# Image line sums on TensorE, low row halves on Pool, token reloads issued at once, in a two-layer MetaFormer kernel

## The chip, the cores and the metric

The kernel runs on one core of a Trainium2 chip. The metric is the time of one execution on the device in microseconds (us), the median of several runs. The engines of the core are TensorE (PE, matmuls; its weight loads are shown as PEld), VectorE (DVE), ScalarE (ACT), GpSimd (POOL, here also called Pool) and SyncE (SP, which here issues most DMAs). They run their own instruction streams and meet only through semaphores.

## The reference

The input x is 16 images of 256 channels and 16 x 16 pixels. Two layers follow each other, each a convolution part and a mixture of experts on the 4096 pixels as tokens:

```
x = x + conv0(ln_c(x))              # ln_c: normed over the channels of a pixel
t = tokens(x)
t = t + ffn0(ln_t(t))               # 8 experts, 2 per token, hidden 512
x = from_tokens(t)
x = x + (weight1 @ ln_c(x) + bias1)
t = t + ffn1(ln_t(t))               # 8 experts, 2 per token, hidden 1024
```

conv0 works on groups of 8 channels. For each group it needs the mean and the maximum of every image row and every image column (`g.mean(axis=3)`, `g.mean(axis=2)` and the same with max), puts them through an 8 x 8 matrix, a bias and a sigmoid, and multiplies the image by the gates of its row and its column, once with the gates from the means (branch r = 0) and once with those from the maxima (r = 1). Statistics of the gated images, a softmax over the group and a mix of both branches follow.

In the experts a token's value is split into two float16 numbers, a high half and a low half (the rest), so that matmuls in float16 keep the accuracy.

## The kernel before

All instructions are written out by hand, engine by engine, with semaphores; the order on an engine is the order of the code. SBUF is laid out by hand too: `tok` holds the 32 token tiles of 128 x 256, `region` and `wreg` are reused from stage to stage.

**First convolution.** PE turns the images to tokens (L674), DVE takes statistics and norms each token tile into one of two buffers `xn` (L1245), PE turns it back (L664), ACT copies it to `g` (L960), channels by pixels: two blocks k of 128 channels, 16 images, 256 pixels. DVE then makes the line sums and line maxima into `line[:, r, k]`, for r = 0 (sum) and r = 1 (max), k = 0 and 1: rows by one reduction (L1273), columns by another (L1275), for r = 0, k = 0 by four additions that fold the image (L1279, L1281). PE multiplies each `line` by the gate matrix (L702), ACT makes the sigmoid (L976) between its sums of squares of expert weights (L968, `squares`). Gating is done in a row part (L256) and a column part (L261), by Pool for (r, k) = (0, 0), (0, 1), (1, 1) and by DVE for (1, 0). Pool starts (0, 0) and (0, 1) with their sigmoids; (1, 1) waits for `signed`, which DVE gives after it has multiplied the maxima's row gates by a sign (L1306). DVE takes `channel_stats` (L1296) of a gated block when it is there, in the order (0, 0), signs, its own gating (1, 0), then (0, 1), (1, 0), maxima (L1299), (1, 1), maxima.

**Between the layers.** Experts add their results to DRAM rows `rows_y`. SP waits for the last of these, reloads `tok` in eight DMAs of 512 KB (L395), of which the fifth to eighth each wait for one of the first four, and then loads raw expert weights (L320, L323). DVE takes statistics of each loaded tile (L1391).

**Second convolution and routing.** PE turns `tok` and multiplies by the weights (L903, L912); Pool adds the bias (L640), DVE adds the result (`result`, L1402) and takes statistics (L1408) for eight groups i of four tiles. `deviations(3, ..)` (L1216 to L1231) makes mean and 1/deviation for one half of the tiles at a time. ACT norms the tiles into `xn1` (L1026) and writes the high halves, scaled by 1024, into `rows` (L1030); `result_lows(i)` on DVE writes the low halves, `xn1 * 1024 - high` (L1415), two instructions per i. DVE does i = 0 to 3 between its results, and i = 4 to 7 after the routing chain (L1469 to L1535) and ahead of the lists (L1545, L1546), which PE sums (L790). ACT makes its rows of i = 4 to 7 behind the exponents of the routing chain. SP stores each i's rows to DRAM when both halves are there. When lists and stores are done, Pool fetches rows for the second layer's experts (L530).

## Time and profile before

| | |
|---|---|
| median of 3 runs | 1151.49 us (1150.26 to 1151.76) |
| profiled execution | 1151.33 us |
| its span in the trace | 1149.6 us |
| PE busy | 878.1 us (76%) |
| DVE busy | 750.4 us (65%) |
| ACT busy | 575.9 us (50%) |
| POOL busy | 503.5 us (44%) |

Busy time is the sum of an engine's instructions; the span runs from the first to the last instruction. A share of the span is an average over stages with different limits, so the rows below are taken from the stages that the change touches: the first convolution (about 5 to 145 us), the reload of tokens (604 to 624 us) and the second convolution with its routing (610 to 723 us).

### The profile page before, as it was taken

Reading aid. Unit: us, or ns where it says so; the run is one execution under the profiler, and the core shown is the slowest. Engines: PE = TensorE matmul, PEld = TensorE weight load, DVE = VectorE, ACT = ScalarE, POOL = GpSimd, SP = SyncE. Lnnn points to the kernel's source line nnn. Section 1 sums busy time; section 2 is a strip of 40 time slices with the busy share of each in tenths; the row PEclk is TensorE's granted clock in tenths of the full one; section 3 lists DMA queues with packets and bytes.
Section 4 is the critical chain, followed back from the end, with each engine's and each line's share of the span. In section 5 each row is a group of like instructions: output and inputs, shape, how many; then the busy total and the mean of one; then the engine's idle time right before and its main releaser. Section 6 shows DMA issues by size and latency. Waiting matters only on the chain.

```text
span 1149.6 us, 25137 instructions
## 1 busy us (share of the span) xinstructions
PE 878.1 (76%) x7033; PEld 740.0 (64%) x7033; DVE 750.4 (65%) x1814; ACT 575.9 (50%) x1246; POOL 503.5 (44%) x412
## 2 busy tenths in 40 slices
PE   5321085874499999999964826599999999999975
PEld 4201064861288888888853712488888888888863
DVE  5899878999544444444446799466766767766540
ACT  4538266884245445444451466354564554655433
POOL 1198000000247667666661410354655655656640
PEclk8655599895599999999996965799999999999996
DMA  8248265784255565555659136656555464434438
GB/s 266 74 146 296 105 199 195 244 282 116 49 135 105 97 101 99 98 101 96 102 91 297 38 110 157 120 127 142 120 101 143 73 146 78 69 73 78 74 59 292
DMA packets 196629, 152.24 MB, mean 132 GB/s; under 512 B 97056, under 2 KB 181480, under 8 KB 196456
## 3 DMA queue, kind: packets, MB, share of 16 engines
q1 hardware_dynamic: 156536, 108.48, 33.1%
q0 software_dynamic: 27472, 38.97, 20.5%
q10 hardware_dynamic: 12576, 4.26, 1.4%
q8 instruction: 20, 0.33, 0.1%
q14 instruction: 25, 0.20, 0.1%
HBM read 92.35 MB, written 39.91 MB: 115 GB/s over the span
## 4 chain that ended last, share of the span: by engine, by line
PE 35%; DMA 25%; DVE 18%; issue 11%; SPq 4%; ACT 3%; DVEq 1%; POOL 1%; ACTq 1%; POOLq 0%
PE bank L857 14%; PE bank L830 12%; DMA columns<-region 8%; DMA region<-rows_x,region 8%; SPq L419 3%; DMA rows_y<-region 3%; PE bank L912 2%; DVE columns L1296 2%; DVE region L1275 2%; DMA tok<-rows_y 2%; DVE region L1273 2%; PE bank L734 2%; DMA wreg<-in_L_ffn_w_dram 1%; DVE wreg L261 1%; PE bank L812 1%
## 5 line engine op out<-in xcount | busy, mean ns | idle before, releaser
L830 PE MATMUL bank<-columns,wreg 128*128 x3360 | 382.8, 274 | 26.9 <-DMA columns<-region 26.8
L830 PEld LDWEIGHTS bank<-columns,wreg 128*128 128x128 f16 x3360 | 330.2, 98 | 68.9 <-issue 28.5
L583 POOL DMA_INDIRECT rows_y<-region x140 | 242.0, 1729 | 161.0 <-ACT region L1172 99.2
L530 POOL DMA_INDIRECT region<-rows_x,region x148 | 155.9, 1053 | 252.2 <-DVE region L1572 141.4
L857 PE MATMUL bank<-wreg,region 128*128 128x256 f16 x1680 | 189.2, 273 | 10.4 <-DVE region L1701 10.3
L857 PEld LDWEIGHTS bank<-wreg,region 128*128 128x128 f16 x1680 | 163.5, 98 | 32.1 <-DVE region L1701 13.4
L1157 ACT ACTIVATE region<-bank,b_t,wreg 128x256 f32<-128x256 f32 x280 | 137.3, 558 | 25.9 <-PE bank L830 25.5
L1706 DVE TENSOR_TENSOR region<-region 128x256 f16<-128x256 f32 x140 | 50.1, 420 | 107.2 <-ACT region L1164 107.2
L1172 ACT ACTIVATE region<-region 128x256 f32<-128x256 f32 x70 | 31.7, 500 | 163.4 <-DVE region L1713 163.4
L1701 DVE SCALAR_TENSOR_TENSOR region<-region,wreg 128x512 f16<-128x512 f32 x140 | 105.2, 751 | 5.0
L845 PE MATMUL bank<-wreg,region 128*128 (+1 forms) x864 | 100.2, 273 | 1.9 <-ACT region L1164 1.9
L1698 DVE TENSOR_SCALAR region<-region,wreg 128x512 f16<-128x512 f32 x140 | 70.5, 503 | 41.5 <-ACT region L1157 41.5
L1152 ACT ACTIVATE region<-bank,fac 128x256 f32<-128x256 f32 x140 | 62.7, 473 | 62.6 <-PE bank L830 61.8
L845 PEld LDWEIGHTS bank<-wreg,region 128*128 128x128 f16 x864 | 84.4, 98 | 12.0 <-ACT region L1164 2.2
L1134 ACT ACTIVATE region<-bank,region 128x256 f32 x72 | 30.2, 470 | 100.5 <-DMA rows_y<-region 83.8
L790 PE MATMUL bank<-columns 128*128 128x160 f16 x128 | 38.7, 313 | 32.6 <-DVE columns L1546 28.2
L1695 DVE SCALAR_TENSOR_TENSOR region<-bank,fac,region 128x256 f32<-128x256 f32 x140 | 58.9, 477 | 7.0 <-ACT region L1152 7.0
L1713 DVE SCALAR_TENSOR_TENSOR region<-bank,wreg,region 128x512 f32<-128x512 f32 x35 | 26.3, 751 | 55.9 <-PE bank L857 38.9
L578 POOL COPY region<-routed 128x4 uint32 x70 | 59.9, 855 | 4.8 <-DMA region<-rows_x,region 3.0
L968 ACT ACTIVATE wreg<-wreg 128x1024 f32<-128x1024 f32 x56 | 58.5, 1051 | 2.0 <-DMA wreg<-in_L_ffn_w_dram 1.6
L1594 DVE SCALAR_TENSOR_TENSOR wreg<-wreg (+1 forms) x68 | 47.7, 747 | 6.8 <-ACT wreg L1109 4.3
L790 PEld LDWEIGHTS bank<-columns 128*128 128x128 f16 x128 | 13.3, 104 | 58.5 <-DVE columns L1546 49.2
(285 smaller groups left out, 1156.0 us busy)
## 6 DMA issues: line engine op xcount, KB each, us to landing
wreg<-in_L_ffn_w_dram SPq DMA_DIRECT2D x112, 512.0 KB, 6.0
rows_x<-region SPq DMA_DIRECT2D x16, 512.0 KB, 6.5
rows_y<-tok SPq DMA_DIRECT2D x16, 512.0 KB, 6.8
tok<-rows_y SPq DMA_DIRECT2D x16, 512.0 KB, 6.8
wreg<-in_x_dram SPq DMA_DIRECT2D x4, 1024.0 KB, 9.4
out_dram<-columns ACTq DMA_DIRECT2D x16, 256.0 KB, 2.4
region<-rows_x,region POOLq DMA_INDIRECT x148, 2.9
columns<-region SPq DMA_TRANSPOSE x148
```

The source lines that it names most:

```text
L530: nc.gpsimd.indirect_dma_start(x_bits[:, b, r, 0:C + 2], None, rows_x[f], bass.IndirectOffsetOnAxis(ap=row_list, axis=0)).then_inc(xr_load ...
L578: nc.gpsimd.tensor_copy(now[:, b], moves[:, bass.ds(2 * t, 2), :]).then_inc(lists_copied[f], 1)
L583: nc.gpsimd.indirect_dma_start(rows_y[f], bass.IndirectOffsetOnAxis(ap=now[:, b, g_, 1:2], axis=0), (y_pair[:, b], y_rows)[f][:, g_, :], N ...
L830: last = pe.matmul(to, block, x_cols[:, bass.ds(b, 1), :, xs_, k, :].rearrange("p j r n -> p (j r) n"), start=(k == 0 and ws_ + xs_ == 0), ...
L845: last = pe.matmul(yb[:, r * C:(r + 1) * C], lhs[:, r * P:(r + 1) * P], w2_of(c, ws_), start=(c == 0 and r == 0 and hs + ws_ == 0), stop=( ...
L857: last = pe.matmul(yb[:, r * C:(r + 1) * C], lhs[:, c, r * P:(r + 1) * P], v_s[:, e % 2, c // 2, 1, ws_, (c % 2) * C:(c % 2 + 1) * C], sta ...
L968: act.activation(chunk_in[:, n % SLOTS], chunk_in[:, n % SLOTS], ACT.Square, accum_out=to).then_inc(summed, 1)
L1152: act.activation(gate_act[:, h, (c % 2) * TILE:(c % 2 + 1) * TILE], zb[c][:, 0:TILE], ACT.Silu, scale=fac[f][:, 0, e:e + 1]).then_inc(silu ...
L1157: last = act.activation(gate_act[:, h, c * TILE:(c + 1) * TILE], zb[h][:, c * TILE:(c + 1) * TILE], ACT.Silu, bias=b1_t[:, e, 2 * h + c:2 ...
L1695: dve.scalar_tensor_tensor(half(hid[:, h], c), zb[c][:, TILE:2 * TILE], fac[f][:, 1, e:e + 1], half(gate_act[:, h], c), ALU.mult, ALU.mult ...
L1698: dve.tensor_scalar(to_hi, gate_act[:, h], fac[f][:, 1, e:e + 1], None, ALU.mult).then_inc(hi_ready[f], 1)
L1701: dve.scalar_tensor_tensor(to_lo, gate_act[:, h], fac[f][:, 1, e:e + 1], to_hi, ALU.mult, ALU.subtract).then_inc(lo_ready[f], 1)
```

## The change

There are three parts.

1. Norming of the first convolution writes all 32 token tiles to one array, `norm_rows`, instead of two turning buffers. The sums of image lines are made by PE: for each block k, image u and half h a matmul with the normed tile as weights and a selector `line_of` of 32 columns (16 rows, 16 columns of the image) as moving data. ACT copies the sums to `line[:, 0, k]`. DVE makes the selector at the start of the program and keeps the maxima alone.
2. `result_lows` moves from DVE to Pool, behind Pool's bias additions, as a plain subtraction. For this ACT writes `xn1` already scaled by 1024, with a `scaled` factor that DVE makes in `deviations(3, ..)`.
3. SP issues all eight token reloads with no wait among them (two semaphores take the place of one, so each load still has its own count), and waits for the last put `y_put[0]` last instead of first.

```diff
+        norm_rows = x_in.rearrange("p b k n -> p (b k n)").rearrange("p (t c) -> p t c", c=C)
+        line_of = region[:, 6144:6208].rearrange("p (h l) -> p h l", h=UT)
...
+        def tokens_in(f, i):
+            return (tok_loaded[i % 4], 16 + 16 * f) if (i < 4) == (f == 0) else (x_loaded[i % 4], 32 + 16 * f)
...
                 for i in range(HB):
...
-                    if i >= 4:
-                        sp.wait_ge(tok_loaded[f][i % 4], 16 + 16 * f)
                     sp.dma_start(tok[:, 4 * i:4 * i + 4, :], rows_y[f][i * 4 * P:(i + 1) * 4 * P].rearrange("(t p) c -> p t c", p=P)
-                                 ).then_inc(tok_loaded[f][i % 4], 16)
+                                 ).then_inc(tokens_in(f, i)[0], 16)
...
-            for waited, each, more in ((y_put[0], 16, 48), (y_put[1], 16, 16), (xr_loaded[0][0], 16, 48), (xr_loaded[1][0], 16, 48)):
+            for waited, each, more in ((xr_loaded[0][0], 16, 48), (xr_loaded[1][0], 16, 48), (y_put[1], 16, 16), (y_put[0], 16, 48)):
...
+            def result_lows(i):
+
+                for j in range(2):
+                    pool.wait_ge(rows_hi[j], HB + i + 1)
+                    at = rows[:, 4 * i + 2 * j:4 * i + 2 * j + UT, :]
+                    nc.gpsimd.tensor_tensor(at[:, :, C:2 * C], xn1[:, i % 4, j], at[:, :, 0:C], ALU.subtract
+                                            ).then_inc(rows_ready[j], 1)
...
+                    for i in range(HB):
+                        result_lows(i)
...
-            pairs(pe, turn_normed)
-
+            for i in range(HB):
+                turn_normed(i)
+
+            pe.wait_ge(lines_known, 1)
+            for k in range(KC):
+                for u in range(NB):
+                    for h in range(UT):
+                        last = pe.matmul(zb[2 + k][:, u * 2 * HW:(u + 1) * 2 * HW], norm_rows[:, UT * u + h, k * P:(k + 1) * P],
+                                         line_of[:, h], start=(h == 0), stop=(h == UT - 1))
+                last.then_inc(lines_known, 1)
             pe.wait_ge(bd_ready, 1)
             for r in range(2):
                 for k in range(KC):
-                    pe.wait_ge(lines_ready, 2 * (r * KC + k) + 2)
+                    if r == 0:
+                        pe.wait_ge(small_ready, 2 + k)
+                    else:
+                        pe.wait_ge(lines_ready, 2 * k + 2)
...
             squares(0, 4)
+            for k in range(KC):
+                act.wait_ge(lines_known, 2 + k)
+                act.activation(line[:, 0, k].rearrange("p b l -> p (b l)"), zb[2 + k][:], ACT.Copy).then_inc(small_ready, 1)
...
                 if s == 3:
-                    dve.scalar_tensor_tensor(m, m, -1.0, r, ALU.mult, ALU.mult).then_inc(half_normed, 1)
+                    chain(dve.tensor_scalar(scaled[:, at], r, XSCALE, None, ALU.mult))
+                    dve.scalar_tensor_tensor(m, m, -1.0, scaled[:, at], ALU.mult, ALU.mult).then_inc(half_normed, 1)
...
+            for h in range(UT):
+                dve.tensor_reduce(line_of[:, h, 8 * h:8 * h + 8], by_row, AX.X, ALU.add)
+                last = dve.tensor_reduce(line_of[:, h, HW:2 * HW], by_column, AX.X, ALU.add)
+            last.then_inc(lines_known, 1)
...
-                for j in range(2):
-                    dve.wait_ge(rows_hi[j], HB + i + 1)
-                    at = rows[:, 4 * i + 2 * j:4 * i + 2 * j + UT, :]
-                    dve.scalar_tensor_tensor(at[:, :, C:2 * C], xn1[:, i % 4, j], XSCALE, at[:, :, 0:C], ALU.mult, ALU.subtract
-                                             ).then_inc(rows_ready[j], 1)
```

On DVE this is the stretch from the gate matrix to the first statistics of a gated block, before. `region` holds the lines, `wreg` the images `g`.

```order
L1265 TENSOR_TENSOR region<-region 128x128
L1273 TENSOR_REDUCE region<-wreg 128x16x16
L1279 TENSOR_TENSOR region<-wreg 128x2048
L1279 TENSOR_TENSOR region<-region 128x16x64
L1279 TENSOR_TENSOR region<-region 128x16x32
L1281 TENSOR_TENSOR region<-region 128x16x16
L1273 TENSOR_REDUCE region<-wreg 128x16x16
L1275 TENSOR_REDUCE region<-wreg 128x16x16
L1273 TENSOR_REDUCE region<-wreg 128x16x16
L1275 TENSOR_REDUCE region<-wreg 128x16x16
L1273 TENSOR_REDUCE region<-wreg 128x16x16
L1275 TENSOR_REDUCE region<-wreg 128x16x16
```

The same stretch on DVE in the changed kernel, to its own gating.

```order
L1307 TENSOR_TENSOR region<-region 128x128
L1314 TENSOR_REDUCE region<-wreg 128x16x16
L1315 TENSOR_REDUCE region<-wreg 128x16x16
L1314 TENSOR_REDUCE region<-wreg 128x16x16
L1315 TENSOR_REDUCE region<-wreg 128x16x16
L1319 TENSOR_SCALAR region<-region 128x1
L1320 TENSOR_SCALAR region<-region 128x1
L1321 TENSOR_TENSOR region<-region 128x1
L1323 TENSOR_TENSOR conv_wt<-wreg,bank 128x2x8
L1330 BN_STATS columns<-wreg 128x6 x16
L1340 TENSOR_SCALAR region<-region 128x16x16 x2
L261 TENSOR_TENSOR wreg<-wreg,region 128x4096
```

The four reductions that are left are the maxima; the statistics (L1330) of Pool's first gated block and the signs (L1340) follow them directly.

On PE, the changed kernel from the small constants to the gate matmuls: L683 are the transposes, L722 the line sums, L732 the gate matmuls, L738 transposes of a later weight.

```order
L708 MATMUL bank<-wreg 128x8 x2
L709 MATMUL bank<-region 128x11
L683 MATMUL bank<-ident,wreg 128x128 x64
L722 MATMUL bank<-region,wreg 128x32 x64
L732 MATMUL bank<-region 128x512 x4
L738 MATMUL bank<-ident,wreg 128x128 x4
```

The 64 line sums, of both blocks k, stand ahead of the first gate matmul.

On Pool, the changed kernel between the two layers' experts: L648 is the bias, L656 the low halves, L538 the second layer's first fetch.

```order
L648 ISA
L648 TENSOR_TENSOR tok<-tok,routed 128x512 x16
L667 AFFINE_SELECT routed<-ones 128x128
L656 TENSOR_TENSOR region<-wreg,region 128x2x256 x16
L538 DMA region<-rows_x,region 128x258 x2
L574 TENSOR_LOAD bounds
```

All sixteen low halves stand behind all bias additions and ahead of the fetch; on DVE nothing is left between the routing chain and the lists.

## Rows read from the trace of the kernel before

**Rows 1.** The page: busy times, and the chain that ended last by engine.

```profile
PE 878.1 (76%) x7033; PEld 740.0 (64%) x7033; DVE 750.4 (65%) x1814; ACT 575.9 (50%) x1246; POOL 503.5 (44%) x412
...
PE 35%; DMA 25%; DVE 18%; issue 11%; SPq 4%; ACT 3%; DVEq 1%; POOL 1%; ACTq 1%; POOLq 0%
```

**Rows 2.** Timeline, 8 to 61 us: start, duration, engine, line, operation, idle before.

```profile
8.73 1.56 DVE L1236 BATCH_NORM_STATS2 st_lg<-tok  x4 [8.73 <-ACT tok L947]
...
41.07 4.42 DVE L1273 TENSOR_REDUCE region<-wreg 128x256 f32<-128x4096 f32 x1 [1.35 <-ACT wreg L960]
...
45.14 1.28 ACT L976 ACT_TABLE_LOAD   x1
...
52.36 0.69 ACT L976 ACTIVATE region<-bank,region 128x512 f32<-128x512 f32 x1 [5.94 <-PE bank L702]
53.22 7.18 POOL L256 TENSOR_TENSOR wreg<-wreg,region 128x4096 f32<-128x4096 f32 x1 [47.80 <-ACT region L976]
54.38 7.06 DVE L1275 TENSOR_REDUCE region<-wreg 128x256 f32<-128x4096 f32 x1
60.48 8.88 POOL L261 TENSOR_TENSOR wreg<-wreg,region 128x4096 f32<-128x4096 f32 x1
```

**Rows 3.** Timeline, 90 to 131 us, DVE and POOL.

```profile
90.80 0.60 DVE L1306 TENSOR_SCALAR region<-region 128x256 f32<-128x256 f32 x2
...
91.43 4.43 DVE L256 TENSOR_TENSOR wreg<-wreg,region 128x4096 f32<-128x4096 f32 x1
91.48 11.42 POOL L256 TENSOR_TENSOR wreg<-wreg,region 128x4096 f32<-128x4096 f32 x1 [6.04 <-DVE region L1306]
...
95.89 11.28 DVE L261 TENSOR_TENSOR wreg<-wreg,region 128x4096 f32<-128x4096 f32 x1
...
102.97 12.91 POOL L261 TENSOR_TENSOR wreg<-wreg,region 128x4096 f32<-128x4096 f32 x1
...
107.10 10.54 DVE L1296 BATCH_NORM_STATS2 columns<-wreg 128x6 f32<-128x256 f32 x32
...
127.11 4.40 DVE L1299 TENSOR_REDUCE region<-wreg 128x16 f32<-128x4096 f32 x1
```

**Rows 4.** Timeline, 605 to 624 us: the first reloads and the last statistics.

```profile
605.26 2.06 SPq L395 DMA_DIRECT2D tok<-rows_y  x4
...
618.80 4.43 DVE L1391 BATCH_NORM_STATS2 st_lg<-tok 128x6 f32<-128x256 f32 x12 [1.01 <-DMA tok<-rows_y]
```

**Rows 5.** The chain that ended last, at 600 us: start, duration, what.

```profile
599.96 4.11 DMA rows_y<-region
```

**Rows 6.** Windows, 616 to 618 us: engines' busy time, PE clock, DMA share, GB/s.

```profile
616.00:618.00 2.00, 2.00 (x12) 1.54 (x10) 1.41 (x4) 0.46 (x1) 2.00 (x3) 1.00 1.10 364
```

**Rows 7.** Timeline, 646 to 724 us, DVE and POOL.

```profile
646.25 1.27 POOL L640 TENSOR_TENSOR tok<-tok,routed 128x512 f32<-128x512 f32 x1 [1.07 <-PE bank L903]
646.26 1.30 DVE L1218 TENSOR_TENSOR st_lg<-st_lg 128x16 f32<-128x16 f32 x1
...
664.20 0.29 POOL L651 TENSOR_SCALAR_AFFINE_SELECT routed<-ones 128x128 f16<-128x128 f16 x1
...
670.16 0.17 DVE L1216 TENSOR_TENSOR st_lg<-st_lg 128x16 f32<-128x16 f32 x1
...
690.21 4.91 DVE L1415 SCALAR_TENSOR_TENSOR region<-wreg,region 128x512 f16<-128x512 f32 x8
...
723.15 1.19 POOL L530 DMA_INDIRECT region<-rows_x,region  x1 [58.66 <-DVE region L1572]
```

**Rows 8.** Groups by line, PE, 0 to 300 us: count, busy us, mean ns.

```profile
L763 PE MATMUL bank<-gate_w,columns 128*128 128x8 f32 x128 | 15.3, 255 | 0.0
```

**Rows 9.** Windows, 40 to 41 us (columns as in rows 6).

```profile
40.00:41.00 1.00, 0.24 (x3) 0.00 (x0) 0.00 (x0) 0.74 (x3) 0.00 (x0) 1.00 0.00 0
```

**Rows 10.** Timeline, 762 to 764 us, experts of the second layer, DVE and POOL.

```profile
762.41 0.81 POOL L578 COPY region<-routed 128x4 uint32 x1
762.62 0.57 DVE L1698 TENSOR_SCALAR region<-region,wreg 128x512 f16<-128x512 f32 x1
```

49 lines of the change are left out of this document (22 added, 27 removed).

## The prediction

> **What bounds the kernel now.** I read the page's busy times first: TensorE (PE) leads with 76% of the span, VectorE (DVE) has 65%, so no engine is full throughout [rows 1]. The chain that ended last says more: only 35% of it is PE. The change touches three stretches, and each has to be read where it stands.
>
> First convolution, 41 to 131 us. DVE works without a pause from 41.07 us: the row and column sums and maxima of the image lines, in pieces of 4.4 and 7.1 us [rows 2]. The sums feed a matmul and a sigmoid, and with that sigmoid Pool starts its first gating at 53.2; one gating is a row part of 7.2 us and a column part of 8.9 us [rows 2]. At 91.4 DVE and Pool both start gating. Here the rows show how the two share an SBUF port: DVE's row part takes 4.43 us from 91.43, Pool's, started 0.05 us later, lasts 11.42 instead of 7.2; DVE's column part lasts 11.28, though it ends 4.2 us after Pool's row part does; and Pool's second part then lasts 12.91 instead of 8.9 [rows 3]. One instruction holds the port to its end, and the other waits all of it. After that DVE has statistics and maxima until 131.5 (16 of them take 5.3 us, 32 take 10.5, a maximum 4.4) [rows 3].
>
> Token reload, 604 to 623 us. The last put lands at 604.1 [rows 5], the first reload is issued at 605.3, and the second four go out only as the first four land. The last of DVE's statistics ends at 623.2 [rows 4], and the DMA engines are full meanwhile (share 1.10) [rows 6].
>
> Second layer's rows and routing, 650 to 723 us. Between 670.16 and 690.2 DVE runs one serial chain of small operations, then the last eight low halves for 4.91 us, then the lists, whose end lets Pool fetch the first rows for the experts at 723.15 [rows 7].
>
> **The change, part by part.**
>
> *Line sums.* That the normed tiles now have 32 places instead of 2 frees DVE of waits for PE, but ScalarE's copy of each turned tile still paces the transposes: 0, at most a few tenths. From DVE go 41.07 to 61.35, 20.3 us of sums; the maxima now run from 41.1 to about 64.1 (2 x (4.4 + 7.1)). Five small operations that build the selector join at DVE's start, under its wait until 8.73 [rows 2]. PE gets 64 matmuls of 32 columns in fp32. An fp32 matmul shows as two records: the nearest group is the router's, 128 records in 15.3 us with 8 columns and weights of the same shape, so 0.120 us each [rows 8]. Our 64 are 128 records, 15.4 us. PE's transposes end at 40.2, at a granted clock of 1.00 (2.4 GHz) [rows 9], and the new matmuls follow at once: done at 55.6. ScalarE then copies (0.7, priced as the sigmoid of the same shape, 0.69), loads the sigmoid table (1.28, no longer in a wait: the copies stand ahead of it) and makes the sigmoid (0.7), and with 0.2 us for handing over Pool starts at 58.5 instead of 53.2 [rows 2]. Both halves of the sums stand ahead of the first gate matmul on PE, so Pool waits for both.
>
> What does DVE's earlier freedom buy? Its statistics of the first gating need that gating: 58.5 + 16.1 = 74.6, to 79.9. Then the two sign multiplications (0.60 us together) [rows 3] meet Pool's second gating, which began at 74.6 and holds the port until 81.8. I take it that they need the port: small f32-to-f16 tensor_scalars do hold Pool up, a Pool copy of 4 elements asked for at 762.41 is over only at 763.22, when DVE's tensor_scalar begun at 762.62 has ended [rows 10]. So signs at 82.4; Pool's column part, waiting since 81.8, goes next until 91.3; only then can DVE start its row part, which stood at 91.43 before. From there everything repeats rows 3. **Term: -0.1 us.** The 20.3 us taken from DVE turn into waiting for Pool. Bounds, a tenth of the 15.4 us either way for the records' length and the handing over: -1.6 and +1.5.
>
> By the Trainium skill, "SBUF — State Buffer", section "Who interferes with whom", a tensor_scalar in a 2-port mode and any DVE instruction with two SBUF inputs keep GpSimd out for the whole instruction, tensor_reduce never. The first half the rows bear out; without it for the signs the sum would be that of rival 2.
>
> *Low halves on Pool.* DVE loses 16 subtractions: eight of 4.91 us together between the chain and the lists, and eight between results, of which PE's pace hides all but those after 668.7 (about 1.4 us). It gains two small multiplications in the deviations, 0.2 us each. So DVE's chain starts at 668.7 and would end at 689.1, 6.0 us before the lists start now (690.21 + 4.91 = 695.1) [rows 7]. But Pool now runs 16 subtractions of 128x512. The nearest row is its bias addition of the same size, 1.27 us, and this very row shows what it does to DVE: DVE's tensor_tensor of 16 elements beside it took 1.30 us, where one at 670.16 takes 0.17 [rows 7]. Pool is free for them at 664.5, when its select is done [rows 7]. Three or four of the first eight run before DVE's chain starts, five in it. The last eight need ScalarE's rows, which it makes behind the exponent in the middle of the chain, so I put all eight into its second half. That is 13 of 16. Of the chain's 18 us of busy time (59 rows of the timeline, the first at 670.16, the last just ahead of 690.21) I count 13 in operations with two SBUF inputs or of tensor_scalar kind; in the rest (reductions, copies from PSUM) Pool may run beside it [rows 7]. A Pool operation that falls anywhere costs between 0.93 (13/18 of it) and 1.27 us; since the first port-using operation follows within 0.4 us, I take 1.15: 13 x 1.15 = 15.0. **Term: -6.0 + 15.0 = +9.0 us.** Bounds: with Pool's cheapest rate, 7.18 us for 4096 elements [rows 2], one is 0.90 and costs 0.65: 13 x 0.65 - 6.0 = +2.5. At 1.30 with nothing hidden, +10.9. The stores of the rows come later too, but Pool's last subtraction ends near 700 and the lists run to about 728, which hides the stores; without that cover they would cost what they outlast the lists.
>
> The page "GPSIMD Engine Reference", section "Elementwise — side-by-side cycle accounting", of the Trainium skill gives about 2.6 cycles per element for two inputs, an estimate of 1.11 us for 512; the term would be some 2 us smaller by it. The 1.27 us of the row decides.
>
> *Token reloads at once, waits in another order.* Between landing (604.1) and issue (605.3) stand three waits that are long met; with the put's own wait last, 0.9 us goes. The full DMA engines leave little for an earlier issue: the first reload's landing moves with the issue, and the last may gain the half-idle stretch in which four were awaited, about 0.9. **Term: -1.8 us**, bounds -0.9 and -3 (DVE's own 32 statistics then bound it). At the end of the kernel the same eight reloads go through the same queue beside the output's stores, which by this share leave no idle time to win: 0, give or take 1.
>
> Sum: -0.1 + 9.0 - 1.8 = +7.1 on the profiled execution's 1151.33 us (its span is 1149.6; the 1.7 around it stay), which is 0.16 below the median of the runs: **1158.4 us**.
>
> **Rivals.**
> 1. *Pool's subtractions cost DVE nothing* (they fit between its operations, or run beside them). Then the low halves give -6.0 and the total is -7.9: 1143.4 us, faster. For it: a third of the chain's time is in operations that need no port, and Pool may find those. Against it: the row of 1.30 us, from the first of the two deviation chains of this stage [rows 7]. It decides where the 13 subtractions cost DVE less than 7.9 us together, 0.6 us each. Chance 0.22.
> 2. *The signs need no port.* DVE makes them at 80 under Pool's row part and is the first in line when that ends at 81.8; the row part comes at 81.8, Pool's column parts wait, and the last maximum ends 6.9 us sooner. Total +0.2: 1151.5 us, the same. For it: no row shows a tensor_scalar of this very shape beside a long Pool operation. Against it: the copy [rows 10]. Chance 0.15.
> 3. *The line sums run at half clock* (1.2 GHz), 0.24 us a record, 30.8 us: Pool starts at 73.9, the total is +22.5: 1173.8 us. For it: no row shows the clock through 15 us of matmuls as short as these. Against it: the clock is 1.00 up to the last transpose, and PE now goes on without a pause [rows 9]. Chance 0.05.
>
> **How the numbers follow.** The forecast has 0.50; its own range is 1149 (all low bounds: -1.6 + 2.5 - 3 = -2.1) to 1163 (all high: 1.5 + 10.9 - 0.9 = +11.5). A remaining 0.08 is for mixtures of 1 and 2. The range leaves out the far half of rival 1, rival 3 and the top of its own: 1146 to 1163. Within 0.2% (2.3 us, about what a measurement of this kernel can tell from no change) lie rival 2 and small parts of the forecast and of rival 1: 0.18. Faster gets most of rival 1 and the mixtures, 0.24; slower the rest, 0.58.
>
> **What would show it.** Line sums: 128 records of about 0.12 us from 40.2 at clock 1.00, Pool's first gating at 58 to 59, DVE idle some 9 us before its first statistics and again for about 9 us before its row part, last maximum near 131. Low halves: small DVE operations of 0.2 to 0.4 us stretched to 1.2 and more from 669 on, the lists about 9 us later than now measured from the reload. Reload: last statistics near 621.4. The prediction is wrong if the stretched operations are few, if Pool's subtraction is well under 1 us, or if DVE's row part starts at 82.

## The result and the profile after

The changed kernel took a median of 1161.4 us (1158.6 to 1164.71, five runs) against 1151.51 us for the kernel before in the same session: a ratio of 1.0078, 95% interval 1.0057 to 1.0100. It is slower, by 9 to 10 us. The profiled execution took 1158.6 us with a span of 1156.7; what follows are differences of starting times in that one execution against the one of before.

The page of after, busy times:

```profile
PE 893.8 (77%) x7161; PEld 759.7 (66%) x7161; DVE 741.5 (64%) x1798; ACT 576.2 (50%) x1248; POOL 521.2 (45%) x428
```

PE has 15.7 us more than in [rows 1], DVE 8.9 less, Pool 17.7 more. DVE loses less than the 30 us of sums (20.3) and subtractions (16 at 0.61) that were taken from it, because what it still does waits longer for the port it shares with Pool, and the wait counts as busy (10.3 us at the signs and 9.1 in the routing chain, both below).

The stretches from one milestone to the next, each the difference of two starting times (the first is from the span's start to the end of the last maximum):

| us | before | after | a_only | b_only | c_only |
|---|---|---|---|---|---|
| start to last maximum | 131.5 | 135.1 | 136.4 | 131.0 | 130.9 |
| to the first reload | 473.8 | 472.9 | 470.8 | 471.9 | 471.2 |
| to the statistics of the first half | 40.6 | 40.1 | 40.2 | 41.1 | 39.9 |
| to the first list | 49.2 | 52.7 | 49.2 | 52.1 | 49.2 |
| to the first fetch | 28.1 | 28.1 | 28.1 | 28.2 | 28.1 |
| to the last reload | 397.8 | 398.7 | 397.5 | 400.0 | 397.9 |
| to the end | 28.6 | 29.2 | 30.1 | 28.7 | 28.7 |

(a_only, b_only and c_only are experiments with one part of the change each.) The two stages of the experts, 473 and 398 us long, differ by 3 us here (over all the kernels below the first of them takes 469 to 479 us) in a way that follows none of the edits. Each kernel has one trace only, and executions of one and the same kernel differ as much: those of before took 1146.1 to 1161.7 us over all sessions. The places that the edits touch are much steadier.

**First convolution.** Windows of after (us, then busy time and number of PE, PEld, DVE, ACT, POOL, the granted clock of PE, DMA share, GB/s):

```profile
38.00:42.00 4.00, 4.00 (x39) 4.00 (x38) 3.08 (x1) 3.93 (x9) 0.00 (x0) 1.00 0.22 73
42.00:46.00 4.00, 4.00 (x29) 4.00 (x29) 4.00 (x2) 0.97 (x2) 0.00 (x0) 0.74 0.96 308
46.00:50.00 4.00, 4.00 (x20) 4.00 (x21) 4.00 (x1) 0.60 (x1) 0.00 (x0) 0.50 0.45 150
50.00:54.00 4.00, 4.00 (x21) 4.00 (x20) 4.00 (x2) 0.00 (x0) 0.00 (x0) 0.50 0.00 0
```

PE works the whole time, nothing but line sums, and yet its granted clock falls from 1.00 (2.4 GHz) to 0.50 (1.2 GHz) at 43.9 us, 6 us after the first of them. At 1.00 it gets through 39 records in 4 us, 0.103 us each; at 0.50 through 20 or 21, 0.19 to 0.20 each. Timeline of after, PE, DVE and POOL:

```profile
37.93 21.92 PE L722 MATMUL bank<-region,wreg 128*128 128x32 f32 x128
...
62.66 7.18 POOL L261 TENSOR_TENSOR wreg<-wreg,region 128x4096 f32<-128x4096 f32 x1 [57.23 <-ACT region L1009]
...
69.92 8.84 POOL L266 TENSOR_TENSOR wreg<-wreg,region 128x4096 f32<-128x4096 f32 x1
...
78.86 5.33 DVE L1330 BATCH_NORM_STATS2 columns<-wreg 128x6 f32<-128x256 f32 x16 [16.75 <-POOL wreg L266]
...
84.11 10.86 DVE L1340 TENSOR_SCALAR region<-region 128x256 f32<-128x256 f32 x2
...
85.98 8.84 POOL L266 TENSOR_TENSOR wreg<-wreg,region 128x4096 f32<-128x4096 f32 x1
...
95.01 4.43 DVE L261 TENSOR_TENSOR wreg<-wreg,region 128x4096 f32<-128x4096 f32 x1
...
95.05 11.41 POOL L261 TENSOR_TENSOR wreg<-wreg,region 128x4096 f32<-128x4096 f32 x1 [0.23 <-DVE region L1340]
...
130.68 4.39 DVE L1333 TENSOR_REDUCE region<-wreg 128x16 f32<-128x4096 f32 x1
```

The 128 records take 21.9 us instead of the 15.4 forecast, and Pool starts at 62.66 (before: 53.22 [rows 2]). DVE stands idle for 16.75 us. Then come two sign multiplications that took 0.60 us in [rows 3] and now are down for 10.86. The first (1.94 us from 84.11) ends at 86.05, when Pool's second row part is over; the second (9.00 us from 85.97) ends at 94.97, when the column part that Pool started at 85.98 is over (94.8). The row parts start at 95.0, and from there all repeats [rows 3], 3.6 us later.

**Reload.** Timeline of after:

```profile
607.92 2.06 SPq L403 DMA_DIRECT2D tok<-rows_y  x4
...
610.83 4.93 SPq L403 DMA_DIRECT2D tok<-rows_y  x4
...
622.71 2.88 DVE L1425 BATCH_NORM_STATS2 st_lg<-tok 128x6 f32<-128x256 f32 x8 [0.94 <-DMA tok<-rows_y]
```

and the chain that ended last, in the same stretch:

```profile
603.62 4.11 DMA rows_y<-region
```

The last put had landed at 607.73 (603.62 + 4.11), so the first reload follows 0.2 us behind it where it took 1.2 before [rows 4, 5]. The second four go out at 610.83, 2.9 us behind the first. From the landing to the end of the last statistics (the next operation of DVE) it takes 17.9 us, before 19.2.

**Rows and routing.** Timeline of after, DVE and POOL:

```profile
666.88 8.93 POOL L656 TENSOR_TENSOR region<-wreg,region 128x512 f16<-128x512 f32 x8
...
671.20 0.21 DVE L1249 TENSOR_TENSOR st_lg<-st_lg 128x16 f32<-128x16 f32 x1
671.45 1.07 DVE L1250 TENSOR_TENSOR st_lg<-st_lg 128x16 f32<-128x16 f32 x1
...
672.56 1.08 DVE L1251 TENSOR_TENSOR st_lg<-st_lg 128x16 f32<-128x16 f32 x1
673.67 1.06 DVE L1252 TENSOR_SCALAR mean<-st_lg 128x16 f32<-128x16 f32 x1
...
674.77 1.07 DVE L1253 SCALAR_TENSOR_TENSOR st_lg<-st_lg 128x16 f32<-128x16 f32 x1
675.88 0.17 DVE L1254 SCALAR_TENSOR_TENSOR st_lg<-st_lg 128x16 f32<-128x16 f32 x1
...
686.43 2.27 POOL L656 TENSOR_TENSOR region<-wreg,region 128x512 f16<-128x512 f32 x2 [10.62 <-ACT region L1063]
686.62 1.05 DVE L1526 TENSOR_TENSOR top<-top,red 128x64 f32<-128x64 f32 x1
```

DVE's chain starts at 671.20. Its first operation takes 0.21, the next four 1.06 to 1.08 where those of before take 0.17 to 0.19 (the chain's first is in [rows 7]): each lies beside one of Pool's first eight subtractions (8.93 us together, so 1.12 each). They start 1.11 us apart where those of before start 0.21 apart: one operation gets through for each subtraction, and each subtraction costs 0.90. When Pool has finished, the sixth takes 0.17 again. With Pool's next pair it starts once more. Laid beside each other, operation by operation, this chain and that of before show 11 stretched, by 9.1 us together, 0.83 each: four under the first eight subtractions, seven under the last eight. The first list comes at 700.7, 29.5 us behind the chain's start, where the chain and DVE's own subtractions took 24.9 before.

### The profile page after: what moved, and what is told of

Same layout as the page of the kernel before. It is cut to its first block, busy times and chain, and to the rows that moved or that the text cites. A ratio compares the mean times of both kernels' runs of the same rounds, so it can differ in the third digit from the quotient of the medians.

```text
span 1156.7 us, 25366 instructions
## 1 busy us (share of the span) xinstructions
PE 893.8 (77%) x7161; PEld 759.7 (66%) x7161; DVE 741.5 (64%) x1798; ACT 576.2 (50%) x1248; POOL 521.2 (45%) x428
## 4 chain that ended last, share of the span: by engine, by line
PE 42%; DMA 19%; DVE 14%; issue 12%; ACT 4%; SPq 4%; POOL 3%; DVEq 1%; ACTq 0%; POOLq 0%
PE bank L860 15%; PE bank L887 14%; DMA columns<-region 5%; DMA region<-rows_x,region 4%; DMA rows_y<-region 4%; SPq L427 3%; PE bank L875 3%; PE bank L942 2%; PE bank L722 2%; DVE columns L1330 2%; PE bank L764 2%; DVE wreg L1663 2%; DMA tok<-rows_y 1%; DVE wreg L266 1%; DMA out_dram<-columns 1%
## 5 line engine op out<-in xcount | busy, mean ns | idle before, releaser
L860 PE MATMUL bank<-columns,wreg 128*128 x3360 | 382.5, 274 | 28.4 <-DMA columns<-region 28.2
L538 POOL DMA_INDIRECT region<-rows_x,region x148 | 155.1, 1048 | 223.7 <-DVE region L1595 112.7
L1190 ACT ACTIVATE region<-bank,b_t,wreg 128x256 f32<-128x256 f32 x280 | 136.7, 559 | 24.6 <-PE bank L860 21.3
L1721 DVE TENSOR_SCALAR region<-region,wreg 128x512 f16<-128x512 f32 x140 | 70.5, 503 | 41.1 <-ACT region L1190 41.0
L1718 DVE SCALAR_TENSOR_TENSOR region<-bank,fac,region 128x256 f32<-128x256 f32 x140 | 61.0, 479 | 15.3 <-ACT region L1185 14.1
L1617 DVE SCALAR_TENSOR_TENSOR wreg<-wreg (+1 forms) x68 | 47.7, 747 | 6.4 <-ACT wreg L1142 4.3
```

The source lines that it names most:

```text
L538: nc.gpsimd.indirect_dma_start(x_bits[:, b, r, 0:C + 2], None, rows_x[f], bass.IndirectOffsetOnAxis(ap=row_list, axis=0)).then_inc(xr_load ...
L860: last = pe.matmul(to, block, x_cols[:, bass.ds(b, 1), :, xs_, k, :].rearrange("p j r n -> p (j r) n"), start=(k == 0 and ws_ + xs_ == 0), ...
L1190: last = act.activation(gate_act[:, h, c * TILE:(c + 1) * TILE], zb[h][:, c * TILE:(c + 1) * TILE], ACT.Silu, bias=b1_t[:, e, 2 * h + c:2 ...
L1718: dve.scalar_tensor_tensor(half(hid[:, h], c), zb[c][:, TILE:2 * TILE], fac[f][:, 1, e:e + 1], half(gate_act[:, h], c), ALU.mult, ALU.mult ...
L1721: dve.tensor_scalar(to_hi, gate_act[:, h], fac[f][:, 1, e:e + 1], None, ALU.mult).then_inc(hi_ready[f], 1)
```

## The experiments

All timed against the kernel before on the same chip. "In us" is the ratio less 1, on 1151.5 us. The interval of each is 2 to 3 us either way, 4 for best and 5 for best_wide, so two rows that differ by less than some 3 to 4 us are not told apart by their times.

| run | median | before there | ratio, 95% interval | in us |
|---|---|---|---|---|
| a_only | 1155.79 | 1151.64 | 1.0048 (1.0026 to 1.0070) | +5.5 |
| b_only | 1154.58 | 1151.64 | 1.0029 (1.0009 to 1.0049) | +3.3 |
| c_only | 1150.24 | 1151.64 | 0.9994 (0.9977 to 1.0012) | -0.7 |
| lows_half | 1162.98 | 1151.64 | 1.0109 (1.0086 to 1.0133) | +12.6 |
| signs_act | 1155.73 | 1152.16 | 1.0029 (1.0004 to 1.0053) | +3.3 |
| signs_split | 1151.39 | 1152.16 | 0.9994 (0.9976 to 1.0012) | -0.7 |
| lows_early | 1157.09 | 1152.16 | 1.0045 (1.0027 to 1.0063) | +5.2 |
| lows_late | 1161.61 | 1152.16 | 1.0089 (1.0067 to 1.0111) | +10.2 |
| best | 1139.19 | 1153.97 | 0.9880 (0.9849 to 0.9912) | -13.8 |
| clows | 1148.68 | 1153.97 | 0.9959 (0.9939 to 0.9979) | -4.7 |
| best_wide | 1136.56 | 1151.76 | 0.9875 (0.9833 to 0.9916) | -14.4 |

**One part each: a_only, b_only, c_only.** The edits are the three parts of the diff alone; the lines that tell them apart are

```diff
+                        last = pe.matmul(zb[2 + k][:, u * 2 * HW:(u + 1) * 2 * HW], norm_rows[:, UT * u + h, k * P:(k + 1) * P],
+                                         line_of[:, h], start=(h == 0), stop=(h == UT - 1))
```

for a_only,

```diff
+                    for i in range(HB):
+                        result_lows(i)
```

on Pool for b_only, and for c_only

```diff
-                    if i >= 4:
-                        sp.wait_ge(tok_loaded[f][i % 4], 16 + 16 * f)
```

> The kernel before with only the first of the three parts of the change: the line sums of the images on TensorE, the low halves on VectorE and the token reloads as before. The prediction's own term for this part is -0.1 us (1151.4); the trace of after, read by differences of starting times, puts it at +3.6 us (1155.1), because the records of the line sums took 0.17 us each instead of 0.12 and Pool's gating began at 62.7 instead of 58.5. In this trace the line sums should end near 59.9 and the last maximum near 135. Rival: the three parts hold each other up only together, and this one alone costs nothing (1151 to 1152).

> The kernel before with only the low halves of the second layer's rows on Pool (with the factor of 1024 taken into ScalarE's scale). The prediction's term is +9.0 us (1160.5). The trace of after puts it at +3.3 us (1154.8): each Pool subtraction holds VectorE up for 0.75 to 0.9 us rather than 1.15, and it adds 9.5 us to the chain of small operations, against 4.8 us of subtractions that VectorE no longer does and 1.3 us ahead of it. Rival: what remains of the loss of after (some 1.4 us at the second experts and in the end phase) belongs to this part too, and it costs 4.7 us or more (1156.2 and up).

> The kernel before with only the token reloads of the second layer issued without waits on each other (other semaphores for the second half, and the put of the first group awaited last). The prediction's term is -1.8 us (1149.7), the trace of after puts it at -1.2 us (1150.3) at the last statistics of the second layer. Rival: the reload of the last phase, which the same part changes, gives back or costs a further 0.5 us or more (below 1149.8 or above 1150.8).

Measured: +5.5, +3.3 and -0.7 us, together +8.1, beside the +9.0 of the whole change. The parts add up, so no interaction is needed. They are the sizes read from the trace of after (+3.6, +3.3, -1.2), not the terms of the prediction. In a_only the line sums take 22.8 us and the last maximum ends at 136.4. The timed +5.5 (interval 3.0 to 8.1) holds the 4.9 us of its trace. For c_only the stretch from the landing to the statistics is 18.2 us against 19.2, 18.9 and 19.0 in before, a_only and b_only: 0.9 us less than their mean, and in after (17.9) 1.1. The timed difference does not tell this from nothing.

**What holds the row part up: signs_act and signs_split.** In signs_act ScalarE makes the signs:

```diff
+            act.wait_ge(sig_ready, KC * 2)
+            act.wait_ge(bd_ready, 2)
+            for k in range(KC):
+                last = act.activation(sig[:, 1, k, :, 0:HW], sig[:, 1, k, :, 0:HW], ACT.Copy, scale=small[:, CG + 3:CG + 4])
+            last.then_inc(signed, 1)
...
-                last = dve.tensor_scalar(sig[:, 1, k, :, 0:HW], sig[:, 1, k, :, 0:HW], sign, None, ALU.mult)
```

> The changed kernel with the two sign multiplications taken from VectorE to ScalarE (a copy with the sign as its scale, straight behind the sigmoids). Theory: in the traces of after VectorE's multiplication waits 10.3 us for Pool's column part to let go of the port, Pool then goes first again with the next part, and VectorE's row part comes at 95.0 us. With the signs ready VectorE asks for its row part at some 84 us, in the middle of Pool's second column part, gets the port at about 86, 9 us sooner, and the last maximum ends 6 to 7 us sooner: near 128.5 against 135.1, the time near 1154.8. Rival: the multiplication was not what held the row part, which comes at 95 again, and the time stays at 1161.

Timeline of signs_act, DVE, ACT and POOL:

```profile
66.00 7.19 POOL L261 TENSOR_TENSOR wreg<-wreg,region 128x4096 f32<-128x4096 f32 x1 [60.57 <-ACT region L1009]
...
77.06 0.91 ACT L1014 ACTIVATE region<-region 128x256 f32<-128x256 f32 x2
...
87.47 6.08 DVE L261 TENSOR_TENSOR wreg<-wreg,region 128x4096 f32<-128x4096 f32 x1
...
89.34 12.89 POOL L266 TENSOR_TENSOR wreg<-wreg,region 128x4096 f32<-128x4096 f32 x1
...
127.74 4.40 DVE L1339 TENSOR_REDUCE region<-wreg 128x16 f32<-128x4096 f32 x1
```

Here the line sums took 24.6 us, so everything starts late and has to be counted from Pool's first gating: from its start to the end of the last maximum it is 66.1 us, against 72.4 in after (62.66 to 135.07). That is 6.3 us less, where 6 to 7 were forecast. DVE's row part is in line at 87.47, has the port when Pool's row part ends at 89.3 (its column part stands at 89.34), and Pool's column part is the one that waits. That is the place whose time the expectation gave (about 86 us in after, where the second row part ends), though it spoke of the column part. The sign multiplication thus needed the port, and cost 6 us. The timed gain over after is 5.7 us (+3.3 against +9.0).

signs_split adds, in the line sums' loop on PE (and alike on ScalarE):

```diff
+                if k == 0:
+                    pe.wait_ge(bd_ready, 1)
+                pe.wait_ge(small_ready, 2 + k)
+                pe.matmul(zb[k][:], conv_bd[:], line[:, 0, k].rearrange("p b l -> p (b l)"),
+                          start=True, stop=True).then_inc(gates_psum, 1)
```

> As the run with the signs on ScalarE, and the gate matmul and sigmoid of the sums of the first 128 channels follow straight after these channels' line sums, instead of after all sums. Theory: Pool starts its first gating about 12 us sooner (some 49 to 51 us against 62.7), VectorE's first statistics at about 67, and the last maximum ends some 17 to 18 us before that of after (near 117), unless VectorE's own row of work (maxima until 61.4, then some 55 us) becomes the bound, which is the same value. The time is near 1144, below the kernel before. Rival: what is gained here is given back in the first experts' stage, since their weights are still being prepared (by ScalarE's squares and by transfers), and less than half of it arrives at the token reload: 1152 or more.

Timeline of signs_split:

```profile
38.38 11.15 PE L722 MATMUL bank<-region,wreg 128*128 128x32 f32 x64
...
52.16 13.70 PE L722 MATMUL bank<-region,wreg 128*128 128x32 f32 x64
...
53.26 7.18 POOL L261 TENSOR_TENSOR wreg<-wreg,region 128x4096 f32<-128x4096 f32 x1 [47.81 <-ACT region L1006]
...
80.44 9.37 DVE L261 TENSOR_TENSOR wreg<-wreg,region 128x4096 f32<-128x4096 f32 x1 [5.49 <-ACT region L1018]
...
121.07 4.40 DVE L1343 TENSOR_REDUCE region<-wreg 128x16 f32<-128x4096 f32 x1
```

Pool starts at 53.26, 9.4 us before that of after but not the 12 forecast, since the first 64 records alone took 11.15 us, most of them at the low clock (0.50 from 42 us on). The last maximum ends at 125.5, 9.6 us before that of after instead of 17 to 18: DVE's row part starts at 80.44 behind a new wait of 5.5 us for ScalarE, which has eight squares ahead of the second pair of sigmoids. A wait removed was in part given to the next one in line. The time is that of the kernel before, so the rival's number came out. Part of the shortfall is this wait, which the rival did not have. The other part is the rival's own mechanism or scatter: of the 9.6 us, 5.3 arrive at the reload (602.6), because the first experts' stage takes 477.1 us in this trace, 472.9 in after. One trace of each, in a stage that varies by as much elsewhere, does not decide between the two.

**What the low halves cost: lows_half, lows_early, lows_late.** In lows_half the last eight subtractions go back to DVE:

```diff
-                    for i in range(HB):
-                        result_lows(i)
+                    for i in range(4):
+                        result_lows(nc.gpsimd, pool, i)
...
+                for i in range(4, HB if f == 1 else 4):
+                    result_lows(dve, dve, i)
                 pairs(dve, lists)
```

> The changed kernel, but the last four groups of low halves (eight of the sixteen subtractions) are done by VectorE again, just ahead of the lists, where the kernel before has them; the first four groups stay on Pool. If the loss of this part is Pool's subtractions lying over the chain of small operations, the chain takes some 20 us again instead of 29.5, VectorE gets back 4.8 us of subtractions, and the time is 4.7 us below that of after (1156.7 against 1161.4). Rival: the chain is slow for another reason and the time rises by the 4.8 us that VectorE takes on (1166).

Neither number came: from the half statistics to the first list it takes 53.0 us, after has 52.7, and the timed runs stand 3.6 us above after (+12.6 against +9.0). The intervals of the two overlap (+9.9 to +15.3, +6.6 to +11.5), and the trace shows only 0.3 us of this at the place of the edit. Timeline of lows_half, DVE and POOL:

```profile
665.35 8.93 POOL L273 TENSOR_TENSOR region<-wreg,region 128x512 f16<-128x512 f32 x8
...
669.92 1.08 DVE L1250 TENSOR_TENSOR st_lg<-st_lg 128x16 f32<-128x16 f32 x1
...
674.35 0.17 DVE L1254 SCALAR_TENSOR_TENSOR st_lg<-st_lg 128x16 f32<-128x16 f32 x1
...
694.65 4.90 DVE L273 TENSOR_TENSOR region<-wreg,region 128x512 f16<-128x512 f32 x8 [1.15 <-ACT region L1063]
```

The last eight, on DVE, take 4.9 us behind a wait of 1.15 us for the rows (my edit let DVE wait for ScalarE's last row before it starts), and the second half of the chain runs undisturbed. But the first eight, on Pool, still stretch four operations (the first of them shown) by 3.6 us, until they end at 674.3. My expectation had put the whole loss on the last eight. Counted by this run, the last eight on Pool cost 5.6 us of stretch (9.1 less 3.6, over seven operations) and save 4.9 on DVE, nearly a draw; the loss is the first eight, which DVE did almost unseen between its results.

lows_early therefore puts these between Pool's bias additions, ahead of the chain:

```diff
                     for i in range(HB):
                         add_bias(i)
+                        if i >= 5:
+                            result_lows(nc.gpsimd, pool, i - 5)
+                    result_lows(nc.gpsimd, pool, 3)
```

> The changed kernel, but Pool's first eight subtractions stand between its bias additions (each group as soon as ScalarE has written it), ahead of VectorE's chain, and the last eight are VectorE's again, ahead of the lists. Theory: what Pool's part cost was each subtraction that lay over the chain of small operations, 0.8 to 0.9 us apiece: four of the first eight (3.6 us) and about seven of the last eight (5.8 us). Here at most one lies over the chain; from the chain's first operation to the first list it takes 25 us (20 of chain, 4.9 of subtractions) instead of 29.5, and the time is 4 to 5 us below after: near 1157. Rival: Pool's subtractions delay its bias additions and so the results by as much, and nothing is gained (1161).

From the half statistics to the first list it takes 47.7 us, 5.0 less than in after (forecast 4.5); the results' stage ahead of it is 0.8 longer. The timed difference to after is 3.8 us (+5.2 against +9.0).

lows_late leaves the last eight on Pool, but behind the chain:

```diff
+                    pool.wait_ge(slots_known, 2)
+                    for i in range(4, HB):
+                        result_lows(nc.gpsimd, pool, i)
```

> As the run before it, but the last eight subtractions are Pool's again and wait until the chain is over, so they lie beside the lists (VectorE operations of 0.25 and 0.31 us that follow each other closely). Theory of the port: a small operation of VectorE waits for each Pool subtraction here too; the chain takes 20 us to the first list, but the lists grow from 28.1 us to 34 or 35, which makes it 1 to 3 us slower than the run before it. Rival: the lists are paced by ScalarE and TensorE, the subtractions cost them nothing, and the whole is 4.9 us faster than the run before it.

The first list comes after 43.5 us instead of 47.7, but the lists until the fetch take 35.2 instead of 28.1: 2.9 us worse together, and 5 us in the timed runs. Beside the lists eight subtractions stretch eight operations, to 1.16 to 1.20 us each, and cost 7.1 us, 0.9 each. It is the port again, at a third place; a gap into which they would fit unseen was not there.

**Line sums and the clock: sums_wide.**

```diff
-                        last = pe.matmul(zb[2 + k][:, u * 2 * HW:(u + 1) * 2 * HW], norm_rows[:, UT * u + h, k * P:(k + 1) * P],
-                                         line_of[:, h], start=(h == 0), stop=(h == UT - 1))
+                        last = pe.matmul(zb[2 + k][:, u % 4 * P:(u % 4 + 1) * P], norm_rows[:, UT * u + h, k * P:(k + 1) * P],
+                                         ident[:], start=(h == 0), stop=(h == UT - 1))
```

> The changed kernel, but the 64 matmuls of the line sums multiply with the whole unit matrix (128 columns instead of 32) and write over each other's places, so the sums are not the image's and what follows works on other numbers; only the stretch of these matmuls is read. In the traces of after and of five variants the 128 records take 21.9 to 25.0 us, at a granted clock that is 0.83 to 1.00 in the first 4 us and 0.50 from about 46 us on, though TensorE has no pause. Theory: it is the form with few columns to each load of weights that the clock falls in, and with 128 columns it stays at or near 1.00, so that four times the columns take about as long (20 to 28 us). Rival: the clock falls in the same way whatever the width, and the records at 0.50 take 0.35 us and more, over 40 us together.

Windows of sums_wide, PE alone (us, busy time and number, granted clock, DMA share, GB/s), and its timeline:

```profile
42.00:46.00 4.00, 4.00 (x38) 1.00 0.97 311
46.00:50.00 4.00, 4.00 (x39) 1.00 0.58 206
50.00:54.00 4.00, 4.00 (x30) 1.00 0.00 0
```

```profile
38.48 14.46 PE L722 MATMUL bank<-ident,wreg 128*128 128x128 f32 x128
```

The clock stays at 1.00, and 128 records of 128 columns take 14.5 us, less than the same number of 32 columns took in any kernel (21.9 to 25.0). At 38 or 39 records in 4 us a record of 128 columns lasts no longer than one of 32 at the same clock (39 in 4 us, in after). Up to these matmuls the two programs are the same. Besides the width, the tile that is read and the places written differ; best_wide below keeps the selector and the places. The run's total (one execution, 1159.9 us) says nothing, since what follows works on other numbers.

**Everything together: best, clows, best_wide.** best has signs_split's edits with the gates of both kinds of the first 128 channels ahead of the squares, and lows_early's low halves:

```diff
+                for r in range(2):
+                    act.wait_ge(gates_psum, 2 * k + r + 1)
+                    act.activation(sig[:, r, k].rearrange("p b l -> p (b l)"), zb[2 * r + k][:], ACT.Sigmoid,
...
+                act.activation(sig[:, 1, k, :, 0:HW], sig[:, 1, k, :, 0:HW], ACT.Copy, scale=small[:, CG + 3:CG + 4]).then_inc(signed, 1)
+                if k == 0:
+                    squares(4, 12)
```

> All that the earlier runs point to, in one kernel: the signs on ScalarE, both gate matmuls and sigmoids of the first 128 channels straight after these channels' line sums, the squares 4 to 11 between the two halves instead of ahead of the second row of sigmoids, the reload as in after, and the low halves as in the run with early Pool subtractions. Theory: in the run with signs and split VectorE waited 5.5 us for the signs behind ScalarE's squares (row part at 80.4, last maximum 125.5); that wait goes, and Pool's port time is the bound: last maximum near 122.7. With the 5.0 us that the early subtractions gave between the half statistics and the lists, the time is near 1144 (ratio 0.993). Rival: the first experts' stage does not follow an earlier start, and the time is 1148 or more.

clows is the kernel before with parts 2 (as in lows_early) and 3, without part 1:

```diff
+                        if i >= 5:
+                            result_lows(nc.gpsimd, pool, i - 5)
...
-                        sp.wait_ge(tok_loaded[f][i % 4], 16 + 16 * f)
```

> The kernel before with the reloads of the change and with the low halves as in the run with early Pool subtractions, but with the line sums on VectorE as before. Theory: the reload gives 1.1 us, the low halves 1.5 us from half statistics to fetch (75.8 against 77.3) less 0.6 in the results' stage, so the time is near 1149.5, and what the run with everything gains beyond it (5 to 6 us) is the line sums' share once their waits are gone. Rival: low halves in this form gain nothing, 1151.

Timeline of best:

```profile
52.79 7.18 POOL L261 TENSOR_TENSOR wreg<-wreg,region 128x4096 f32<-128x4096 f32 x1 [47.36 <-ACT region L1006]
...
116.32 4.39 DVE L1336 TENSOR_REDUCE region<-wreg 128x16 f32<-128x4096 f32 x1
```

The last maximum ends at 120.7, 10.8 us before that of the kernel before and 2 sooner than forecast. The time is 13.8 us (10.1 to 17.4) below before, more than the 7.5 forecast. The touched places of its trace hold 12.1 us of it (10.8 at the last maximum, 1.3 from the first reload to the first fetch). The execution that was traced is the slowest of the six (1146.0 us): in it the experts' stages took 3.8 and 1.8 us more than in before, which this trace can't explain. clows gives -4.7 us where -2 was forecast. Between the two lie 9 us: the worth of the line sums on PE together with the signs on ScalarE and the gates half by half. No run has these last two with the sums on DVE, so how much of the 9 is the sums' own is not shown; alone, as in a_only, they cost 5.5.

best_wide widens the selector with zero columns:

```diff
+                        wide = P if u < NB - 3 else 2 * HW
+                        last = pe.matmul(zb[2 + k][:, u * 2 * HW:u * 2 * HW + wide], norm_rows[:, UT * u + h, k * P:(k + 1) * P],
+                                         line_of[:, h, 0:wide], start=(h == 0), stop=(h == UT - 1))
```

> The combined kernel, with the selector of the line sums widened by zero columns from 32 to 128, for 13 of the 16 images (the additional columns land in the places of the next images, whose own matmuls then write over them; the last three images keep 32). From the run with 128 columns, where the 128 records took 14.5 us at a granted clock of 1.00 throughout, against 10.8 + 13.7 us in the combined kernel. Theory: the width holds the clock up here too; the first half takes some 7.3 us, Pool starts at about 49.3 instead of 52.8, the second half is done by 61 and its gates no longer make Pool wait 1.7 us, and the last maximum ends 3.5 to 5 us sooner, at 116 to 117; the time is near 1135. Rival: it was the ones of the unit matrix, not the width, that held it, since zero columns are little work; then the two halves take 24 us again or more and the time is 1139 or above.

Windows of best_wide, PE alone, and its timeline:

```profile
46.00:50.00 4.00, 1.10 (x2) 0.92 0.49 171
50.00:54.00 4.00, 3.49 (x10) 0.50 0.00 0
54.00:58.00 4.00, 4.00 (x29) 0.73 0.51 137
58.00:62.00 4.00, 3.43 (x32) 1.00 0.90 264
```

```profile
38.10 7.23 PE L724 MATMUL bank<-region,wreg 128*128 128x128 f32 x64
...
48.14 7.18 POOL L261 TENSOR_TENSOR wreg<-wreg,region 128x4096 f32<-128x4096 f32 x1 [42.70 <-ACT region L1007]
...
52.38 9.05 PE L724 MATMUL bank<-region,wreg 128*128 128x128 f32 x64
...
112.10 4.40 DVE L1337 TENSOR_REDUCE region<-wreg 128x16 f32<-128x4096 f32 x1
```

The first 64 records take 7.2 us (10.8 in best), Pool starts at 48.14, the last maximum ends at 116.5: as forecast. A unit matrix or zeros in the added columns make no difference to these 64 (half of the 14.5 us above). The second half starts at 0.50, behind a window in which PE was busy for 1.1 of 4 us, and the clock comes back to 1.00 at 56.2 us, while the wide records run (29 in the window at 0.73, 32 at 1.00); in best it stayed at 0.50 through the same half (64 records of 32 columns, 13.7 us). In time best_wide (-14.4) can't be told from best (-13.8); both beat both kernels.

## Why the prediction was right, and which of its terms were not

**The result.** 1161.4 us lies in the range, 3.0 above the forecast, and on the side that had most of the chance. But that was luck: the sum was right because two large errors had opposite signs. -0.1 + 9.0 - 1.8 was forecast, +5.5, +3.3 and -0.7 were measured part by part.

**Line sums (forecast -0.1, measured +5.5 timed, +3.6 and +4.9 in two traces).** The step that failed is "so 0.120 us each ... 15.4 us". The mean of the router's records in [rows 8] was taken for a stretch that those records never form, and the tenth that I allowed either way was far too narrow: 0.17 us on the mean, 21.9 to 25.0 us in all. The trace of before shows what is behind that mean. Timeline of PE, and windows (columns as in [rows 6]):

```profile
204.76 2.31 PE L763 MATMUL bank<-gate_w,columns 128*128 128x8 f32 x16
...
232.16 1.85 PE L763 MATMUL bank<-gate_w,columns 128*128 128x8 f32 x16
```

```profile
204.50:206.50 2.00, 2.00 (x16) 2.00 (x14) 2.00 (x4) 1.02 (x2) 0.00 (x0) 0.70 0.35 115
230.00:234.00 4.00, 3.65 (x33) 3.65 (x34) 4.00 (x11) 3.42 (x6) 0.00 (x0) 1.00 1.03 285
```

The 128 records stand in eight runs of 16. Seven take 1.85 us and one, in which the clock was at 0.50 for its first records, 2.31; there they start 0.21 us apart, in the others 0.11. So 0.120 was the price at 1.00, and at 1.00 the line sums kept it (0.103). What failed is the silent step that the clock of the last transpose would hold for 15 us of these records. Rival 3 had the mechanism (the clock falls to half) but at 0.24 us a record and from the first on; the rows show 0.19 to 0.20, and only from 41 to 44 us on. Its chance of 0.05 was too small, with no row of such a stretch to exclude it. Of the steps behind it these held: both halves of the sums stand ahead of Pool; Pool's second column part goes ahead of DVE's row part; the row part comes last. The signs were thought to be done ahead of that column part (82.4 us); the second of them had to wait through it, to the same effect. signs_act shows that the signs' need of the port costs 6.3 us, of which rival 2 spoke. By the Trainium skill, "SBUF — State Buffer", section "Who interferes with whom", a tensor_scalar in a 2-port mode is kept out for the whole of a Pool instruction and a reduction is never: the traces agree with both. The signs took 10.86 us, and a reduction over columns beside Pool's first gating took 7.06 us [rows 2], where in after, with Pool idle, it took 6.98.

**Low halves (forecast +9.0, measured +3.3).** The -6.0 was right: 4.9 us of subtractions, and a start of the chain that is 1.2 us earlier, counted from the half statistics. The step "13 x 1.15 = 15.0" was not: 11 operations were held up, by 0.83 us each, 9.1 together. The price was the larger error. A subtraction takes 1.12 us and not the 1.27 of the bias addition, and the operation that gets through beside each would have taken its 0.21 us anyway, so about 0.9 is left. The count was too high by two: four of the first eight and seven of the last eight hold an operation up. The bounds (+2.5 to +10.9) held it. Rival 1 is excluded by the five stretched rows above and by b_only. That the price is that of Pool's subtractions lying over DVE's operations was tried at three places: it is 3.6 us for the first eight under the chain, gone in lows_early, and 7.1 us for eight beside the lists. Not every operation pays it: the copy from PSUM at 687.59 us in after lies wholly beside a subtraction and takes 0.41 us, as in before (0.42).

**Reloads (forecast -1.8, measured about -1.1 in traces, -0.7 timed and not told from 0).** The 0.9 at the issue came (0.2 us from landing to issue instead of 1.2). The step that failed is the further 0.9 at the last landing, "the half-idle stretch in which four were awaited": from the first reload's issue to the end of the last statistics it takes 18.0 us in before and 18.0 in c_only, 17.7 in after and 17.7 in a_only, whose reloads are those of before.

**Open.** In the traces the last stretch, from the last reload to the end, is 28.9 to 30.1 us in nine of the ten kernels with line sums on PE (28.8 in best_wide) and 28.6 or 28.7 in the four without; no row showed me why. The first experts' stage takes 469 to 479 us from trace to trace with no edit in it, and I did not find why. With one trace of each kernel this may be the scatter between executions. It is why a gain of a few us at the last maximum can't be followed to the end of a single trace, and why the timed runs carry the verdicts.

## What to carry to other kernels

Work that moves off a busy engine pays only if nobody waits for it at its new place: the sums cost 5.5 us on TensorE as they were. With the gates behind them issued half by half and the signs off the shared port, the kernel came out 9 us below the one with none of the three. Beside a chain of small VectorE operations each Pool subtraction of 1.12 us costs 0.8 to 0.9 us, since it lets one of them through; put such work where VectorE waits or reduces. When a term leans on the mean of one group of records, ask at which granted clock that group ran and whether a long stretch of the new records would keep it.

## What the runs showed of the hardware that was not expected

TensorE's granted clock fell to 0.50 while it worked without a pause, in all eight kernels whose line sums have 32 columns (128 fp32 records, 21.9 to 25.0 us together; the first 4 us at 0.83 to 1.00, the fall 2.6 to 6.0 us after the first record). With 128 columns, from the unit matrix or filled up with zeros, it stayed at 1.00 through 14.5 and 7.2 us and rose to it once from 0.50, in one trace each; the same number of records took 14.5 us: four times the columns, at least a third less time. Why the clock goes with the width is not shown. A Pool subtraction of 128x512 that writes float16 took 1.12 us, an addition of the same size that writes float32 1.27; what makes the difference was not tried.
